# Four 64x64 tiles for the distances, first loads moved ahead of the last stores, strip buffers in other places

## The reference, cut to what matters

```python
x = x + _L0_conv_ref(_gn(x), ...)     # a small U-net of 3x3 convolutions, strides and deconvolutions
x = x + _L1_conv_ref(_gn(x), w_off, b_off, w_def)   # a deformable 3x3 convolution

def _L1_conv_ref(x, w_off, b_off, w_def):
    offsets = _conv2d(x, w_off, b_off, STRIDE, PAD)      # 18 channels: dy, dx of nine taps
    return _deform_conv(x, offsets, w_def, STRIDE, PAD)

# in _deform_conv, per tap k and pixel:
py = hs + iy + dy
px = ws + ix + dx
# bilinear value of x at (py, px), zero outside, then
return jnp.einsum('bckhw,ock->bohw', val, w_def.reshape(Cout, C, K2))
```

## Time and profile before

| | us |
|---|---|
| median of 3 runs | 1393.29 |
| lowest and highest | 1391.19, 1394.08 |
| the profiled execution, its own time | 1396.72 |
| span of the profiled execution | 1394.9 |
| PE busy in the span | 1153.4 (83%) |
| DVE busy | 895.4 (64%) |
| ACT busy | 670.8 (48%) |
| POOL busy | 58.1 (4%) |
| offsets of the second image done on PE | about 771 |
| first samples of strip 0 on PE | 834.07 |
| last strip's sum on DVE | 1380.65 |

### The profile page before, as it was taken

How to read it: one execution, slowest core, us unless ns; L and a number is a source line. 1 busy time by engine, 2 the same in 40 slices (tenths; PEclk the granted TensorE clock), 3 DMA queues, 4 the chain that set the end, 5 groups by cost and what they waited for, 6 DMA issues and landing times.

```text
span 1394.9 us, 38923 instructions
## 1 busy us (share of the span) xinstructions
PE 1153.4 (83%) x15570; PEld 635.0 (46%) x15570; DVE 895.4 (64%) x1380; ACT 670.8 (48%) x901; POOL 58.1 (4%) x86
## 2 busy tenths in 40 slices
PE   0799999965918999999659149999999988898995
PEld 0253346742313554476424015555555555554554
DVE  4868651428838786514288067888877867786880
ACT  0532432012535324320126246888867867786871
POOL 0000000000330000000004200000000000000000
PEclk9999999997968999999979568999999999999998
DMA  9000012204660001122044442333333333333341
GB/s 184 1 1 1 13 76 62 63 1 121 155 177 4 1 2 37 52 62 63 1 121 108 138 118 68 107 100 109 106 110 96 106 109 106 94 104 108 106 122 39
DMA packets 94702, 109.99 MB, mean 79 GB/s; under 512 B 12591, under 2 KB 81839, under 8 KB 92864
## 3 DMA queue, kind: packets, MB, share of 16 engines
q1 hardware_dynamic: 86064, 102.11, 27.3%
q10 hardware_dynamic: 8464, 5.37, 1.7%
HBM read 75.22 MB, written 32.22 MB: 77 GB/s over the span
## 4 chain that ended last, share of the span: by engine, by line
issue 48%; PE 36%; DVE 5%; DMA 3%; ACT 3%; POOL 2%; SPq 2%; ACTq 0%; POOLq 0%; DVEq 0%
PE psum L799 21%; PE psum L868 12%; DMA xm<-x 2%; DVE v L1588 1%; PE psum L909 1%; SPq L513 1%; DMA offd<-offp 1%; PE psum L932 1%; POOL offr L1964 1%; POOL offp L1968 1%; ACT xm L1337 1%; PE psum L890 1%; DVE xm L1754 1%; PE psum L899 1%; DVE stats L1757 0%
## 5 line engine op out<-in xcount | busy, mean ns | idle before, releaser
L799 PE MATMUL psum<-v,u 64*64 64x512 f32 x3072 | 337.3, 597 | 17.6 <-DVE v L1588 12.7
L1409 ACT ACTIVATE dist<-psum 128x1024 f32<-128x1024 f32 x288 | 288.9, 1023 | 103.8 <-PE psum L990 98.4
L1801 DVE TENSOR_SCALAR dist<-dist 128x1024 f32<-128x1024 f32 x288 | 199.3, 692 | 118.4 <-ACT dist L1409 115.1
L799 PEld LDWEIGHTS psum<-v,u 64*64 64x64 f32 x3072 | 151.7, 134 | 201.6 <-issue 176.8
L1034 PE MATMUL psum<-hat,win 64*64 64x144 f32 x4096 | 194.1, 327 | 17.3 <-DMA win<-pixd 14.2
L1810 DVE TENSOR_TENSOR hat<-dist 128x512 f32<-128x512 f32 x288 | 194.6, 684 | 0.3
L990 PE MATMUL psum<-offs,sels 128*128 128x512 bf16 x576 | 175.7, 398 | 19.1 <-issue 15.4
L1034 PEld LDWEIGHTS psum<-hat,win 64*64 64x64 f32 x4096 | 144.9, 138 | 79.5 <-issue 78.2
L1107 PE MATMUL psum<-val,wdefs 64*64 64x256 f32 x1944 | 161.4, 397 | 18.7 <-ACT val L1412 13.4
L1412 ACT ACTIVATE val<-psum 128x864 f32<-128x864 f32 (+3 forms) x230 | 146.5, 674 | 36.2 <-PE psum L1034 25.9
L1107 PEld LDWEIGHTS psum<-val,wdefs 64*64 64x64 f32 x1944 | 74.8, 134 | 70.9 <-issue 61.0
(11 more groups left out here) (144 smaller groups left out, 1087.5 us busy)
## 6 DMA issues: line engine op xcount, KB each, us to landing
win<-pixd SPq DMA_DIRECT2D x256, 68.0 KB
win<-pixd SPq DMA_DIRECT2D x128, 136.0 KB
raw<-x SPq DMA_DIRECT2D x16, 512.0 KB, 7.7
x1d<-xm SPq DMA_DIRECT2D x16, 512.0 KB, 6.0
pixd<-turned SPq DMA_DIRECT2D x64, 128.0 KB, 5.0
x1t<-x1d SPq DMA_DIRECT2D x128, 64.0 KB, 2.3
out<-outt SPq DMA_DIRECT2D x126, 64.0 KB, 2.0
offd<-offp SPq DMA_DIRECT2D x16, 384.0 KB
```

The source lines that it names most:

```text
L799: mm = pe.matmul(o, u4[half, i, v, ky, :], V[half, at:at + CHUNK, cg, v, :], start=start, stop=stop, skip_group_check=True)
L1409: act.activation(dist_at(j, n), psum[:, slot:slot + 2, :], ACT.Abs).then_inc(dist_abs, 1)
L1801: dve.tensor_scalar(d, d, 1.0, 1.0, ALU.min, ALU.subtract).then_inc(hats_made, 1)
```

## The change

**Distances.** The rows of `offs` are laid out anew: each half of the image has its own 61 rows (54 of offsets, 7 of constants) at partition 0 or 64. A distance, before two matmuls of 128 rows, 128 columns and 512 values, becomes eight of 61 rows, 64 columns and 256 values, one for each axis, half and image. `side_of` puts image 1's halves the other way round, so that the four matmuls of an axis fall on the four quarters of the array. x and y of one image now share a PSUM bank, and the product on DVE reads them from there. `sels` shrinks to half. The edge distances change in the same way.

**Order of loads.** For the second image SP runs `last_image`. `sels` and `wdefs` are loaded before the first pixel store. After the fourth `store_pixels` and the fourth `store_parts` comes `first_strips`: it waits until DVE is through with the normalized image (`rows_free`), loads eight pieces of constants, waits for the first four parts, and loads `offs` slot 0, the windows of strips 0 and 1, and `offs` slot 1. The last four `store_pixels` and `store_parts` follow, then the waits for everything, and `load_x1`.

**Places.** The strip buffers lie over tiles from which nothing is stored any more at that time; `freed` and the three waits for it are gone. The clearing of `val` moves from DVE to POOL.

```diff
+        def side_of(b, h):
+
+            return h if b == 0 else 1 - h
+
...
             def sampling_constants():
 
+                sp.wait_ge(even_made, IMAGES * STEPS_OF)
+                sp.dma_start(sels[:], sel).then_inc(sel_in, 16)
+                sp.dma_start(wdefs[:], wtaps).then_inc(sel_in, 16)
+
+            def first_strips(b):
+
                 sp.wait_ge(rows_free, 4 * IMAGES + 4)
                 sp.wait_ge(x1_out, MARGIN + IMAGES * 8 * 16)
...
+                for i in range(SLOTS):
+                    sp.wait_ge(parts_out[i], MARGIN + (b * 32 + 16))
+                sp.wait_ge(pads_in, IMAGES * 32)
+                load_offs(0, 0)
+                for i in range(2):
+                    sp.wait_ge(pm_out[i], MARGIN + (b * 128 + 64))
+                for margin in MARGIN_SEMS[3:]:
+                    sp.wait_ge(margin, MARGIN)
+                for j in range(2):
+                    load_windows(0, j)
+                load_offs(1, 1)
...
+                sampling_constants()
+                store_pixels(b, 0)
+                store_pixels(b, 1)
+                store_parts(b, 0)
+                store_pixels(b, 2)
+                store_parts(b, 1)
+                store_pixels(b, 3)
+                store_parts(b, 2)
+                store_parts(b, 3)
+                first_strips(b)
+                store_pixels(b, 4)
+                store_pixels(b, 5)
+                store_parts(b, 4)
+                store_pixels(b, 6)
+                store_parts(b, 5)
+                store_pixels(b, 7)
+                store_parts(b, 6)
+                store_parts(b, 7)
...
-            sp.sem_inc(freed, 1)
             for j in range(2):
                 load_x1(0, j)
...
                     pe.wait_ge(dist_abs, UNITS * s + (n - 1))
+                    settled(pe)
                 lo = HALF_W * (PS * (r + 1) + 1 - ky)
                 for axis in range(2):
-                    mm = pe.matmul(psum[:, 2 * dist_slot(j, n) + axis, :].rearrange("p (b n) -> p b n", b=IMAGES),
-                                   sels[:, 2 * n + axis, :], offs[:, slot, :, lo:lo + PS * HALF_W], start=True, stop=True)
+                    for h in range(2):
+                        for b in range(IMAGES):
+                            of, to = slice(CH * h, CH * h + SEL_K), CH * side_of(b, h)
+                            dst = psum[to:to + CH, 2 * dist_slot(j, n) + b, PS * HALF_W * axis:PS * HALF_W * (axis + 1)]
+                            mm = pe.matmul(dst, sels[of, 2 * n + axis, :], offs[of, slot, b, lo:lo + PS * HALF_W], start=True,
+                                           stop=True, skip_group_check=True)
                 mm.then_inc(dist_made, 1)
...
-            pe.wait_ge(freed, 1)
             settled(pe)
             quad(0, 0, 0, 0, first=True)
...
-            dve.wait_ge(freed, 1)
-            dve.memset(val[:, 1], 0.0).then_inc(val_cleared, 1)
             strip_step(0, 0, 1)
+            dve.wait_ge(val_cleared, 1)
             strip_step(1, 1, 1)
...
+            pool.wait_ge(edge_dist, 1)
+            pool.memset(val[:, 1], 0.0).then_inc(val_cleared, 1)
             pool.wait_ge(strip_sum, STRIPS + 1)
```

More of the change, by code:

```diff
@@ L254, in build @@
         assert max(high.at, turn.at) <= m.at
[L257 to L267 removed]
+        in_x = Map(X_AT)
+        offs = in_x("offs", [P, 2, IMAGES, OFF_COLS], BF16)
+        win = in_x("win", [P, 2, IMAGES, WINDOWS, CH])
+        x1t = in_x("x1t", [P, 2, IMAGES, HALF_STRIP])
+        assert in_x.at <= U4_AT
+        in_u4 = Map(U4_AT)
+        sels = in_u4("sels", [P, 2 * TAPS, CH], BF16)
+        wdefs = in_u4("wdefs", [P, TAPS, CH])
+        outt = in_u4("outt", [P, 2, IMAGES, HALF_STRIP])
+        hat_e = in_u4("hat_e", [P, 4 * EDGE_PITCH])
+        assert in_u4.at <= WOFF_AT
+        in_stage = Map(STAGE_AT)
+        dist = in_stage("dist", [P, DIST_RING, 2, BANK])
+        assert in_stage.at <= V_START
+        past_offsets = Map(low.at)
+        hat = past_offsets("hat", [P, 2, (TAPS + K) * TAP_PITCH])
+        val = past_offsets("val", [P, 2, TAPS * PS, VAL_PITCH])
         m3 = Map(maps_start)
@@ L306, in build @@
         rows_free = sem("rows_free")
-        freed = sem("freed")
         raw_added = sem("raw_added")
@@ L672, in _ @@
                 image(b, next_x)
-            image(IMAGES - 1, next_stage)
+            last_image(IMAGES - 1)
             sp.wait_ge(x1_out, MARGIN + (IMAGES * 8 * 16))
@@ L998, in edge_distances @@
                     for kx in range(K):
-                        dst = psum[:, axis, W0 * kx:W0 * kx + W0].rearrange("p (b x) -> p b x", b=IMAGES)
-                        mm = pe.matmul(dst, sels[:, 2 * (2 * K * e + kx) + axis, :], offs[:, e, :, lo:lo + HALF_W], start=True,
-                                       stop=True)
+                        at = HALF_W * (K * axis + kx)
+                        for h in range(2):
+                            for b in range(IMAGES):
+                                of, to = slice(CH * h, CH * h + SEL_K), CH * side_of(b, h)
+                                mm = pe.matmul(psum[to:to + CH, b, at:at + HALF_W], sels[of, 2 * (2 * K * e + kx) + axis, :],
+                                               offs[of, e, b, lo:lo + HALF_W], start=True, stop=True, skip_group_check=True)
                 mm.then_inc(edge_dist, 1)
@@ L1415, in take_group @@
                 if g == ACT_GROUPS[0]:
-                    if isinstance(s, int) and s < 1:
-                        act.wait_ge(freed, 1)
-                    else:
+                    if not (isinstance(s, int) and s < 1):
                         act.wait_ge(strip_conv, 4 * s)
-                    settled(act)
+                        settled(act)
                 act.wait_ge(vals_made, GROUPS * s + (g + 1))
@@ L1983, in selectors @@
 def selectors():
-    s = np.zeros((P, TAPS, 2, 2, WIN * WIN), np.float32)
+    s = np.zeros((2, CH, TAPS, 2, WIN * WIN), np.float32)
     wy = np.concatenate([np.repeat(np.arange(WIN), n) for _, _, n in WIN_PARTS])
@@ L1990, in selectors @@
         ky, kx = divmod(k, K)
-        for h in range(2):
-            for part in range(PARTS):
-                at = HALF_K * h + OFFC * part
-                s[at + 2 * k + 1, k, 0, h] = 1.0
-                s[at + 2 * k, k, 1, h] = 1.0
-            s[CONST_AT + 1 + K + K * h + kx, k, 0, h] = 1.0
-        s[CONST_AT + 1 + ky, k, 1] = 1.0
-        s[CONST_AT, k, 0] = HALO - wx
-        s[CONST_AT, k, 1] = HALO - wy
-    return s.reshape(P, 2 * TAPS, P).astype(np.dtype("bfloat16"))
+        for part in range(PARTS):
+            s[:, OFFC * part + 2 * k + 1, k, 0] = 1.0
+            s[:, OFFC * part + 2 * k, k, 1] = 1.0
+        s[:, HALF_K + 1 + K + kx, k, 0] = 1.0
+        s[:, HALF_K + 1 + ky, k, 1] = 1.0
+        s[:, HALF_K, k, 0] = HALO - wx
+        s[:, HALF_K, k, 1] = HALO - wy
+    return s.reshape(P, 2 * TAPS, CH).astype(np.dtype("bfloat16"))
 def ramps():
     rows = PS * (QUAD + 2)
-    r = np.zeros((P - CONST_AT, rows, HALF_W), np.float32)
-    r[0] = 1.0
+    r = np.zeros((2, CONSTS, rows, HALF_W), np.float32)
+    r[:, 0] = 1.0
     for ky in range(K):
-        r[1 + ky] = ((np.arange(rows) + ky - 1) % PS)[:, None]
-    r[1, PS] = -1.0
-    r[K, PS * QUAD + 3] = PS
+        r[:, 1 + ky] = ((np.arange(rows) + ky - 1) % PS)[:, None]
+    r[:, 1, PS] = -1.0
+    r[:, K, PS * QUAD + 3] = PS
     for h in range(2):
```

73 lines of the change are left out of this document (30 added, 43 removed).

## The result

The changed kernel takes **1373.54 us** (median of four runs, 1368.57 to 1380.54), the kernel before beside it 1393.66. The ratio is 0.986, 95% interval 0.983 to 0.989, so the change gains 20.1 us, where 31.5 were forecast (1393.29 less 1361.8). The profiled execution of the changed kernel took 1373.18 us and spans 1371.4, 23.5 less than the 1394.9 of before. In what follows spans are compared with spans.

A forecast was written before the change was run, and what follows sets the result against it. SP's queue of DMA issues, not PE, was taken to bound the loop over strips 4 to 27. The profiled 1396.72 less 27.4 and 4.1 gave 1365.2, or 1361.8 from the median 1393.29; range 1352 to 1374.

The forecast's parts named there:

- What bounds the kernel: Loop over strips 4 to 27: SP's unbroken issues bound it at 17.66 us a strip, not PE at 15.8.
- Term 1: Front, until SP issues the first load of x1t: forecast at 827.7 us (828.31 before), bounds 823 to 838.
- Term 2: From load_x1 to the loop: SP waits for almost nothing, so the loop begins at 884.8, 27.4 us earlier.
- Term 3: Loop over strips 4 to 27: stays at 422.6 us on SP, no gain, 1.5 either way.
- Term 4: Behind the loop: PE arrives in time for strip 31's windows, 4.1 us gained, the rest as before.
- PE's gain: Rival, loop: SP's issues become shorter, strips go at 14.3, 79 us more, 1283 (partly: near 1320); chance 0.07.
- The narrow matmuls: Rival, distances on PE: the eight matmuls run one after another, 1.06 us a distance, 97 slower, 1459; chance 0.05.
- The turn-over: Rival, front: pixel stores collide with window reads and part stores, landings long, load_x1 at 840 to 848, 1374 to 1383; chance 0.10.

The follow-up runs named there:

- e7: Changed kernel with SP's waits for the end of the first stage moved from ahead of load_x1 to ahead of the loop: 1365.95 us, ratio 0.9794.
- e6: Kernel before, with the stores of outt and the loads of x1t moved from SP's queue to POOL's: 1374.90 us, ratio 0.9867.
- e5: Changed kernel with the stores of outt and all loads of x1t moved from SP's queue to POOL's: 1330.74 us, ratio 0.9539.

## Why the prediction was right, and where it missed

The measured 1373.54 lies 11.7 us above the forecast of 1361.8 and only 0.5 inside the range of 1352 to 1374. What gives the gain and what gives none was right. That the time still fell into that range is partly luck: single runs of the changed kernel spread over 12 us.

**What bounds the kernel: right.** Four kernels with PE busy for 1070 to 1151 us sum their strips at 17.11 to 17.18 us each, the kernel before too. With 96 issues more they go at 19.70, with eight of SP's issues a strip given to POOL at 15.2 to 16.3. Only "without a hole" was too strong: the two holes at the turns of the loop, some 3 us each, are in both kernels.

**Term 1, load_x1: 3.6 us late** (831.30 for 827.7, inside its bounds). Two steps were mis-sized. The fourth part landed later than the 9.9 I took: its store, second of the two that start at 760.24, let SP go at 773.51 instead of 771.0. My upper end, 12.4, was the better row. The second twelve loads of offsets took 5.5 instead of 4.5. Windows (15.5 for 15.8), pixels (6.4 for 6.0) and the second landing (817.73 + 1.17 to 831.30, 12.4, where 12.4 and 0.7 for the row of waits were taken) were right.

**Term 2, load_x1 to the loop: 3.8 us late** (60.9 for 57.1). The mechanism held: SP waits for nobody, strip 0 is sampled at 798.49 (near 800 forecast) and summed at 835.68, and strip 1's second group is held until then. But I priced a written-out strip with 12.93 from the one behind the loop, and the four ahead of it took (892.22 - 836.67) / 4 = 13.9. The excess is in single calls: four loads of x1t in 3.59 instead of 2.51, four stores in 2.96, windows in 8.39. e7 shows such calls too in those strips. What makes such a call dearer isn't settled. Behind the loop, where SP pauses as little, the same strip took 12.9 in one kernel and 13.6 in the other, so the lack of a pause is not the whole cause.

**Term 3, the loop: right in kind.** Forecast unchanged, 418.8 after 422.6 on SP, more than the 1.5 either way that I allowed, and by the sums 0.4 us in all. The 3.8 has no cause that a run shows: e1, with the quarters alone, has 422.2 on SP (911.17 to 1333.40), and e2, with the order alone, 421.1 (889.24 to 1310.34). My price of 17.6 for a strip is SP's and was too high for the engines, who begin the loop with windows ready; that didn't touch this sum, but it spoiled the expectation of e6. I had PE waiting for windows in most strips, 3 us each. There were 13 such waits in 24 strips, 45.5 us in all, and 36.6 of that in the five that follow loads of offsets.

**Term 4, behind the loop: wrong**, +0.3 for -4.1. The step that failed is that strip 31 starts when its windows have landed and the rest stays as before. SP issued the last windows from 1324.61 to 1332.33, so they were there at about 1334.6, and PE came at 1336.50: 1.9 late, where it had been 4.1 late, since a strip cost it 13.6 us from 1322.88 on even at its new price. That leaves 2.2. The stand for instructions took 2.1 of it back, and the written-out strip ahead cost SP 13.6 instead of 12.9. So PE was still late for the last windows, and the rest did not stay as before.

```profile
1332.57 1.52 PE L1154 MATMUL psum<-val,wdefs 64*64 64x256 f32 x24 [1.22 <-issue]
...
1336.50 5.55 PE L1081 MATMUL psum<-hat,win 64*64 64x144 f32 x112
```

Together 3.6 + 3.8 - 3.8 + 4.4 = 8.0 us of the missing span. By the sums of the strips the same miss falls otherwise: strip 4 came 25.9 us earlier for the 27.4 forecast of the loop's start, and from strip 28 to the end it took 64.2 us instead of 61.4, where 4.1 less were forecast. So part of the 3.8 that term 2 lost and term 3 won is a matter of where SP stands ahead of the engines, and term 4 was the larger miss. The other 3.4 between 31.5 and 20.1 are no mechanism: the prediction carried the distance of the profiled execution from its median (1396.72 against 1393.29) over to the changed kernel, whose profiled execution lay at its median.

**The rivals.** PE's gain didn't come through, not even in part that can be measured. The narrow matmuls do overlap: a distance takes 0.22 to 0.28 us, at the low end of the 0.25 to 0.35 taken. (Half of the 0.53 is 0.27, not 0.22, and the floor of 0.23 was set a little too high.) The turn-over went a little worse than taken, far from 840. Of the prediction's conditions for being wrong, a loop under 415 or load_x1 outside 820 to 840, neither came about, and neither did the third, a distance over 0.73 us.

## What to carry to other kernels

Before pricing what a busy engine saves, count the issues of the queue that feeds it: a queue with an empty list of waits and hardly a hole between its calls was the bound here, even beside an engine that is 92% busy. Then a change of the engine is worth nothing until issues are taken off that queue, and the same edit that gave 0 to 7.5 us here gave 30.6 once they were. When a stage's price is read off a queue or an engine that starts it with a lead, read it a second time off the last engine of the chain.

## What the runs showed of the hardware

- In this loop an issue more on SP's queue costs about 0.73 us, pauses between groups of calls included (96 of them cost 70.3 us). Four stores take 2.64 us for 128 bytes each and 2.63 for 64 KB each, so the size is not what is paid. POOL's queue issued the same rows at 0.57 to 0.59 us each, where four on SP took 2.5 to 2.6, 0.62 to 0.66 each, and issues from both queues went side by side (groups of e5: busy, mean ns):

```profile
L544 POOL DMA_DIRECT2D out<-outt x126 | 73.7, 589 | 316.9 <-DVE outt L1903 315.2
...
L533 POOL DMA_DIRECT2D x1t<-x1d x126 | 70.2, 566 | 7.1 <-issue 5.0
```

- Eight matmuls of 64 columns and 256 values on the four quarters keep PE for 0.22 to 0.28 us, where two of 128 columns and 512 values kept it for 0.53.
- In a run of very short matmuls PE can stand for its own instructions: 1.6 to 2.4 us over the kernels that show it, at a place that 64 instructions, added at a point some 570 us earlier, move by 16 matmuls.
